# Layer-0 output projection over five slices of the contraction instead of eight

## The reference, cut to what matters

```python
Wdkv = x @ latent_w + latent_b                      # (b, t, 36): one latent, keys and values at once
q = jnp.einsum('btc,hcl->bhtl', x, Wd_w) + Wd_b[None, :, None, :]       # 16 heads of 36
scores = jnp.einsum('bhtl,bsl->bhts', q, Wdkv) / jnp.asarray(np.sqrt(d_head), dtype=x.dtype)
attn = jax.nn.softmax(jnp.where(causal[None, None, :, :], scores, -jnp.inf), axis=-1)
y = jnp.einsum('bhts,bsl->bhtl', attn, Wdkv)
z = jnp.transpose(y, (0, 2, 1, 3)).reshape(b, t, h * Wdkv.shape[-1])    # 16 * 36 = 576 columns
return z @ out_w + out_b                            # the projection that the change is about
```

## Time and profile before

| | us |
|---|---|
| median of 3 runs | 1982.03 (1975.81 to 1985.0) |
| the profiled execution | 1975.02 |
| its span, first to last instruction | 1973.3 |
| PE busy in the span | 1603.3 |
| DVE busy in the span | 1138.7 |
| time from one step of the loop to the next | 23.47 |

### The profile page before, as it was taken

How to read it: one execution, slowest core, us unless ns; L and a number is a source line. 1 busy time by engine, 2 the same in 40 slices (tenths; PEclk the granted TensorE clock), 3 DMA queues, 4 the chain that set the end, 5 groups by cost and what they waited for, 6 DMA issues and landing times. The chain is left out here.

```text
span 1973.3 us, 43060 instructions
## 1 busy us (share of the span) xinstructions
PE 1603.3 (81%) x13932; PEld 1192.2 (60%) x13933; DVE 1138.7 (58%) x2540; ACT 963.6 (49%) x2418; POOL 895.2 (45%) x1484
## 2 busy tenths in 40 slices
PE   4799999999999999989959999999999994212120
PEld 3656656565566665579948888888888883202020
DVE  3365555555555555434428999999999996211110
ACT  3354555555555455534427777877777782000000
POOL 5234444444444444434444444444444431556542
PEclk8599999999999999999979999999999997555555
DMA  8222122212212211322201111111111114323213
GB/s 228 64 40 43 41 43 49 44 40 40 40 40 41 42 41 40 63 57 67 65 24 40 42 35 39 37 37 38 37 41 35 39 35 92 70 42 60 43 19 91
DMA packets 185520, 99.83 MB, mean 51 GB/s; under 512 B 98946, under 2 KB 176323, under 8 KB 182211
## 3 DMA queue, kind: packets, MB, share of 16 engines
q1 hardware_dynamic: 173698, 83.54, 18.9%
q0 software_dynamic: 11776, 15.75, 3.9%
HBM read 64.98 MB, written 37.91 MB: 52 GB/s over the span
## 5 line engine op out<-in xcount | busy, mean ns | idle before, releaser
L611 POOL TENSOR_SCALAR_AFFINE_SELECT probs<-probs 128x512 f32<-128x512 f32 x256 | 173.9, 702 | 197.7 <-ACT probs L1444 197.5
L1444 ACT ACTIVATE probs<-bankT 128x1024 f32<-128x1024 f32 x128 | 131.0, 1023 | 221.0 <-PE bankT L1763 221.0
L893 DVE TENSOR_REDUCE mneg<-bankS 128x2 f32<-128x256 f32 x256 | 109.0, 426 | 212.6 <-PE bankS L1743 210.9
L894 DVE TENSOR_REDUCE mneg<-bankS 128x2 f32<-128x512 f32 x256 | 174.6, 682 | 0.0
L1435 ACT ACTIVATE qT<-bankA,bd 128x256 f32<-128x256 f32 x256 | 107.5, 473 | 87.7 <-PE bankA L1725 87.7
L2137 PE MATMUL bankB<-ident,xg 128*128 128x128 f32 x32 | 8.7, 427 | 173.3 <-DMA xg<-xtab,sidx 173.3
L1725 PE MATMUL bankA<-xnT,wd 128*128 128x256 f32 x512 | 148.9, 414 | 0.0
L604 POOL CAST qb<-qT 128x256 bf16<-128x256 f32 x256 | 97.1, 398 | 96.9 <-ACT qT L1435 96.7
L1777 PE MATMUL bankB<-probs,vaug 128*64 128x512 f32 x512 | 139.0, 621 | 1.2 <-POOL probs L611 0.8
L1760 PE MATMUL bankT<-qT,kT 37*128 37x512 f32 x512 | 136.9, 611 | 3.2 <-ACT probs L1446 2.0
L821 POOL DMA_INDIRECT acc<-yo,aidx x64 | 91.7, 1433 | 102.0 <-DMA acc<-yo,aidx 90.7
(11 more groups left out here) (302 smaller groups left out, 4516.0 us busy)
## 6 DMA issues: line engine op xcount, KB each, us to landing
rzb<-reciprocals SPq DMA_DIRECT2D x64, 384.0 KB, 5.4
xtab<-tab SPq DMA_DIRECT2D x32, 192.0 KB, 2.0
xs_sorted<-zeros SPq DMA_DIRECT2D x1, 4608.0 KB, 19.1
qT<-xs_sorted SPq DMA_DIRECT2D x36, 128.0 KB, 2.1
ys_sorted<-qT SPq DMA_DIRECT2D x36, 128.0 KB, 1.8
value_rows<-vrow SPq DMA_DIRECT2D x32, 128.0 KB, 1.8
vx<-value_rows SPq DMA_DIRECT2D x256, 16.0 KB, 1.9
acc<-res SPq DMA_DIRECT2D x32, 128.0 KB, 1.8
```

What stands on the lines that cost most here:

```text
L611: pool.affine_select(out=blocks, in_=blocks, compare_op=ALU.is_ge, fill=0.0, base=0, pattern=[[0, 4], [1, P]], channel_multiplier=-1).then ...
L893: dve.tensor_reduce(mneg[:, n.half, 0, :, j], bankS[:, :, 0:128], AX.X, ALU.max, negate=True)
L894: dve.tensor_reduce(mneg[:, n.half, 1, :, j], bankS[:, :, 128:384], AX.X, ALU.max, negate=True).then_inc(S["red_done"], 1)
L1444: act.activation(pT[:, g % 2].rearrange("p e j t -> p e (j t)"), bankT[:, 0:2, :], ACT.Exp, scale=SCALE0).then_inc(S["exp_done"], 1)
```

## The change

The contraction of the projection has 576 rows of weights plus one for the bias, which would fill 4.5 tiles of 128; before, it is done over 8 tiles of which 74 rows each carry something. Now it is done over 5 (`FULL`). Pairs 0 to 4 stay where they are. The rows of pairs 5, 6 and 7 (six heads) are copied by DMA, before they are normalised, from their own place into the empty rows 37 to 63 and 101 to 127 of tiles 0 to 4. `MOVES` lists six such copies, three for each half: 27 rows of three pairs, 9 rows of two pairs, and 9 rows of one pair. The weights `ow` are laid out in the same way. The bias moves to tile 4.

The inverses are laid out likewise: two broadcasts to the 37 native rows of each half (5 KB on each partition), and one for each entry of `MOVES`. So a batch now has six copies within SBUF and eight broadcasts of `rzb`, in place of two broadcasts. SP issues the copies two at a time in the round trip (`move`), and DVE waits for all 14 transfers on one semaphore (`zrows_in`). `normalise` covers 5 tiles in three instructions instead of 8 in four, and `outp` has 5 matmuls for a token tile instead of 8.

The loads of `ow` at the start stand behind those of x now and count on `w_in`, which PE waits for ahead of its loop.

```diff
+        FULL = 5
+        REST = PAIRS - FULL
+        NATIVE = (slice(0, L + 1), slice(LP, LP + L + 1))
+        W27 = LP - (L + 1)
+        MOVES = []
+        for e in range(2):
+            o = LP * e
+            MOVES.append((slice(o, o + W27), slice(FULL, PAIRS), slice(o + L + 1, o + LP), slice(0, REST)))
+            MOVES.append((slice(o + W27, o + L), slice(FULL, FULL + 2), slice(o + L + 1, o + 2 * L + 1 - W27), slice(REST, FULL)))
+            MOVES.append((slice(o + W27, o + L), slice(FULL + 2, PAIRS), slice(o + 2 * L + 1 - W27, o + 3 * L + 1 - 2 * W27), slice(REST, REST + 1)))
+        ow = sb("ow", [P, FULL, C])
...
+            def move(p, k):
+                for rows, heads, to, tiles in MOVES[2 * k:2 * k + 2]:
+                    sp.dma_start(yT[to, p.half, tiles, :], yT[rows, p.half, heads, :]).then_inc(S["zrows_in"], 16)
+
             def denominators_out(p):
                 sp.wait_ge(S["y_sb"], p.b * GROUPS + GROUPS)
                 sp.dma_start(den_d, yT[DEN:DEN + LP + 1:LP, p.half]).then_inc(S["den_out"], 16)
+                sp.wait_ge(S["zrows_in"], p.b * NZ)
+                move(p, 0)
                 sp.wait_ge(S["den_out"], p.b * 16 + 16)
                 sp.dma_start(dq[:, :], den_d.rearrange("e j t -> (e j t)").rearrange("(p k) -> p k", p=P)).then_inc(S["den_in"], 16)
+                move(p, 1)
 
             def reciprocals_out(p):
                 sp.wait_ge(S["rec_done"], p.b + 1)
                 sp.dma_start(rec_d.rearrange("e j t -> (e j t)").rearrange("(p k) -> p k", p=P), rq[:, :]).then_inc(S["rec_out"], 16)
+                move(p, 2)
 
             def reciprocals_in(p):
                 sp.wait_ge(S["rec_out"], p.b * 16 + 16)
                 for e in range(2):
-                    sp.dma_start(rzb[LP * e:LP * e + RB], rec_d[e:e + 1].to_broadcast([RB, PAIRS, T])).then_inc(S["rzb_in"], 16)
+                    sp.dma_start(rzb[NATIVE[e]], rec_d[e:e + 1, 0:FULL].to_broadcast([L + 1, FULL, T])).then_inc(S["zrows_in"], 16)
+                for rows, heads, to, tiles in MOVES:
+                    e = rows.start // LP
+                    sp.dma_start(rzb[to, tiles], rec_d[e:e + 1, heads].to_broadcast([to.stop - to.start, heads.stop - heads.start, T])).then_inc(S["zrows_in"], 16)
...
             def normalise(p, i):
                 if i == 0:
-                    dve.wait_ge(S["rzb_in"], p.b * 32 + 32)
-                rows = yT[:, p.half, 2 * i:2 * i + 2, :]
-                ins = dve.tensor_tensor(rows, rows, rzb[:, 2 * i:2 * i + 2, :], ALU.mult)
-                if i == GROUPS - 1:
+                    dve.wait_ge(S["zrows_in"], p.b * NZ + NZ)
+                tiles = slice(2 * i, min(2 * i + 2, FULL))
+                rows = yT[:, p.half, tiles, :]
+                ins = dve.tensor_tensor(rows, rows, rzb[:, tiles, :], ALU.mult)
+                if i == FULL // 2:
                     ins.then_inc(S["z_done"], 1)
...
-                for j in range(PAIRS):
+                for j in range(FULL):
                     ins = pe.matmul(bankB[:, t * C:(t + 1) * C], yT[:, p.half, j, t * P:(t + 1) * P], ow[:, j, :],
-                                    start=(j == 0), stop=(j == PAIRS - 1))
+                                    start=(j == 0), stop=(j == FULL - 1))
```

More of the change, by code:

```diff
@@ L160, in program @@
         lwr = sb("lwr", [P, LR])
-        ow = sb("ow", [P, PAIRS, C])
+        FULL = 5
[9 more added lines that the diff above has]
+        ow = sb("ow", [P, FULL, C])
         xn = sb("xn", [P, 2, 2, C])
@@ L175, in program @@
         yT = sb("yT", [P, 2, PAIRS, T])
-        rzb = sb("rzb", [P, PAIRS, T])
+        rzb = sb("rzb", [P, FULL, T])
         dq = sb("dq", [P, H * T // P])
@@ L278, in program @@
         xt_ps xt_act xt_dve rk_sb scats xnT_sb kv_ps kv_sb
-        q_ps q_sb s_ps red_done mT_ps mT_sb st_ps exp_done av_done y_sb den_out den_in rec_done rec_out rzb_in z_done out_ps xa_done cst dumped passed xs_zero rt ex0 rk_ps staged scat0 scat1 te_done xs_in0 xs_in1 w1_sb xsT_ps xsT_sb h_ps h_act h_dve
+        q_ps q_sb s_ps red_done mT_ps mT_sb st_ps exp_done av_done y_sb den_out den_in rec_done rec_out zrows_in z_done out_ps xa_done cst dumped passed xs_zero rt ex0 rk_ps staged scat0 scat1 te_done xs_in0 xs_in1 w1_sb xsT_ps xsT_sb h_ps h_act h_dve
         yt_ps yt_sb ys_out0 ys_out1 te_go w1_in pads
@@ L291, in passed @@
             eng.sem_inc(S["passed"], 1)
-        NA = 2 * 4 + 4 + 3
-        NW = 2 + 2 * KF + 1
+        NA = 2 * 4 + 4
+        NO = 2 * 4 + 1
+        NW = 2 + 2 * KF + 1 + NO
+        NZ = 16 * (len(MOVES) + 2 + len(MOVES))
         FIRST = 4
@@ L314, in _ @@
             sp.dma_start(lbr[:, L:LR], a["L0_ffn_br"].rearrange("(o l) -> o l", o=1).to_broadcast([P, E0])).then_inc(S["w_a"], 16)
[L315 to L318, removed]
             for k in range(1, len(SPANS)):
@@ L321, in _ @@
                 sp.dma_start(xa_all[:, rows, :], xv[:, rows, :]).then_inc(S[f"x_in{k}"], 16)
+            oh = a["L0_attn_out_w"].rearrange("(j e l) c -> e l j c", e=2, l=L)
+            for e in range(2):
+                sp.dma_start(ow[LP * e:LP * e + L, :, :], oh[e, :, 0:FULL]).then_inc(S["w_in"], 16)
+            for rows, heads, to, tiles in MOVES:
+                lo = rows.start % LP
+                sp.dma_start(ow[to, tiles, :], oh[rows.start // LP, lo:lo + rows.stop - rows.start, heads]).then_inc(S["w_in"], 16)
+            sp.dma_start(ow[DEN:DEN + 1, FULL - 1, :], a["L0_attn_out_b"].rearrange("(o l) -> o l", o=1)).then_inc(S["w_in"], 16)
             for e in range(2):
@@ L1032, in step @@
                     normalise(p, 2)
-                    normalise(p, 3)
             first, second = Batch(0, 0), Batch(0, 1)
@@ L1086, in _ @@
             red(Batch(1, 0), 7)
-            for k in range(GROUPS):
+            for k in range(FULL // 2 + 1):
                 normalise(first, k)
@@ L1143, in _ @@
                 tile_step(1, q, 8)
-                normalise(last, q)
+                if q <= FULL // 2:
+                    normalise(last, q)
             with dve.Fori(2, TILES // 4 - 1) as i:
@@ L1880, in _ @@
             step(second, Batch(1, 0), None, Batch(1, 1), True, ranks=True)
+            pe.wait_ge(S["w_in"], 16 * NW)
             with pe.Fori(1, LOOP) as i:
@@ L1887, in _ @@
                 outp(Batch(LOOP, 0), t, B * GROUPS)
-            pe.wait_ge(S["w_in"], 16 * NW)
             pe.wait_ge(S["te_done"], 2)
```

## The result

The changed kernel takes 2343.74 us, median of 4 runs (2336.53 to 2348.9), against 1978.92 for the kernel before (4 runs). The ratio is 1.1848, with a 95% interval of 1.1824 to 1.1872. The forecast was 2350. All of the loss is in layer 0's attention and its tail: the span grew by 369.3 us (1973.3 to 2342.6), and the first multiplication of the last batch came 371.1 us later (1238.18 against 867.11 in the earlier trace rows).

The account below looks back on a forecast made before the run. PE was taken to bound the kernel. 29 steps of 11.9 us (9.4 waiting, 2.5 clock) make 345; with 5, 7 and 11 that is 368 on 1975, and 7.0 to the median gives 2350 us; range 2200 to 2570.

Parts of the forecast that it names:

- Part 1: PE's projection: 6 of 16 matmuls go, saving 1.40 us of 3.73 for each batch.
- rival with spread rows: Native `rzb` transfers spread over a dozen engines or more: PE keeps nearly 1.4 us a step, 1939 us; chance 0.13.
- Part 2: Copy issues on SP in the round trip: hidden, nothing taken, 0.1 us as the upper bound.
- Part 3: Native `rzb` broadcasts: all 74 rows on one engine, 14.8 us, everything landed at S+24.9.
- What is late next: PE at pair 6's row maxima waits for DVE; 8.0 us from landing to next projection, step 9.4 us longer.
- The clock: PE's clock halves after its stand in nearly every step: 5 us of work at half speed loses 2.5 us.
- The sum: Whole kernel: 29 steps of 11.9 us make 345, plus 5, 7 and 11 for batches 0, 30, 31: 368 us.
- The last two batches: Batches 30 and 31: +7 us at PE's projection and +11 us, with sorted rows queueing behind the broadcasts.
- Two different engines: Each native `rzb` broadcast on its own engine: landed S+17.5, step 25.5 us, 2040 us; chance 0.03.
- Half clock all step: PE at half clock throughout each step: up to 44 us of PE work, +20 a step, 2590 us; chance 0.05.
- The crowd's price: Native `rzb` rows at 0.45 us each, 33 us in place of 14.8: 522 us more, 2870 us; chance 0.02.

Follow-up runs that it names:

- even form: The changed kernel with the two native `rzb` broadcasts to 36 rows instead of 37, plus one transfer for both denominator rows: 1936.49 us, 1935.36 when repeated.
- run without copies: The even form without the six copies of `yT` rows, six heads left out of the projection: 1930.90 us, 1938.59 when repeated.
- filled stand: The changed kernel with 24 more matmuls, product unread, where PE stands ahead of the row maxima of pair 6: 2290.25 us.
- half dose: The changed kernel with one native broadcast to 36 rows plus a transfer for its denominator row, the other still on 37: 2144.65 us.
- `RB` = 40: The kernel before with its two `rzb` broadcasts to 40 rows in place of 48: 1977.54 us, ratio 1.0001.
- `RB` = 37: The kernel before with its two `rzb` broadcasts to 37 rows in place of 48: 2599.87 us, one run.
- `RB` = 38: The kernel before with its two `rzb` broadcasts to 38 rows in place of 48: 2245.99 us, one run.

## Why the prediction was right, step by step

**Part 1, right.** The projection went from 3.73 to 2.39 us, 1.34 by these rows, and the even form's step is shorter by 1.40 in one window and 1.30 in the mean. The 43 us of the rival with spread rows are the 41 to 44 us that the even form gained in its two jobs. The change does what it was thought to do; one number of rows hides it.

**Part 2, wrong by half a microsecond a step.** I forgot the issue of `rec_out` itself, and the copies cost 0.75 us each to issue, not 0.68. `rec_out` starts at 617.02, two copies end at 618.91, and `rzb` goes out at 618.95: 1.93 us in place of 1.46. The run without copies shows that they are the cause: 1.47 us there (529.64 to 531.11). So `rzb` is issued at S+7.44, not S+6.92 (S, the start of the projection, is 611.51 here). In the even form the same delay is there (535.28 to 537.21) and costs nothing. I had called it hidden, and in this kernel it is on the path. The first two copies delay `dq` as well, by more than the 0.06 us of the forecast: it goes out 2.37 us behind the denominators (612.01 to 614.38) where 1.82 stood (521.84 to 523.66, and again 1.82 without copies). In the loop the reciprocal is not wanted sooner and this 0.55 us is hidden; at batch 30 it is not. The fence at the head of the copies was not free in one place either: for batch 31 SP sent the denominators at 1195.20 and the copies only at 1202.71, when the `rzb` of batch 30 had landed. DVE's reciprocal of that batch, at 1215.75, did not wait for `dq`, so I count nothing for it.

```profile
1195.20 0.56 SPq L358 DMA_DIRECT2D denominators<-yT  x1
1202.71 1.53 SPq L354 DMA_DIRECT2D yT<-yT  x2
```

**Part 3, right.** One engine, the same for both; 18.04 us from issue to landing against 18.0 (2.3 + 14.8 + 0.9). Before the run it rested on even shares in three transfers and on the rule that the prediction cites; 37, 38 and 40 rows have since shown even shares here.

**What is late next, right.** Landing at S+25.5 against S+24.9, nearly all of the difference from part 2. PE resumed 1.77 us behind it; I had 2.0.

**The clock, too dear.** 1.8 to 2.0 us a step, not 2.5. The fall came in the stand as I had said, but the half clock lasted for 4 us of work behind it, not 5, and was over well before the projection.

```profile
629.30:642.70 13.40, 3.94 (x18) 1.42 (x18) 3.25 (x6) 0.42 (x1) 0.90 (x2) 0.50 0.03 13
642.90:646.50 3.60, 3.60 (x28) 2.34 (x25) 2.02 (x6) 1.20 (x3) 0.00 (x0) 1.00 0.00 0
```

3.94 us of PE work at half speed lose at most 2.0.

**The sum, right, with errors that cancel.** By the starts of the first multiplication:

| | before | after | more | forecast |
|---|---|---|---|---|
| batch 0 | 142.28 | 144.53 | 2.3 | 5 |
| batch 0 to 1 | 17.58 | 34.21 | 16.6 | 11.9 |
| batches 1 to 29, 28 steps | 658.53 | 989.51 | 331.0 (11.82 each) | 333 |
| batch 29 to 30 | 21.33 | 34.47 | 13.1 | 9.9 |
| batch 30 to 31 | 27.39 | 35.46 | 8.1 | 8.1 |

A step is 11.82 us longer against 11.9, and two errors cancel in it. The run with the filled stand separates them: its mean step of 33.34 is 9.82 above 23.52, where I had 9.4 without the clock, and the clock's part is 2.0, where I had 2.5.

The two lines of batch 0 belong together, 18.9 against 16.9. Its `rzb` took 18.39 us, as forecast, but was issued at 126.14, 3.7 us sooner than before; that is not the change's doing (the last section shows it). Behind it stands a wait that I had not seen. SP issues the weights of the next stage right behind the `rzb` of batch 0, from 130.26 to 151.45, 21.2 us, where it took 11.7 before (130.70 to 142.41). The same four issues, before and after:

```profile
133.54 2.98 SPq L366 DMA_DIRECT2D wv<-in_L_attn_wv  x4
```
```profile
138.17 6.36 SPq L392 DMA_DIRECT2D wv<-in_L_attn_wv  x4
```

So the row maxima of the next batch go out at 151.69 and not at 143.27, and PE stands 3.60 us for them. In the kernel before with 37 and 38 rows the four take 9.90 and 10.43 us, in the even form 2.67, so it goes with the few engines. That SP then waits for room in its queue is my reading; no view shows the queue's depth. The forecast had such a wait only in the upper end of its range.

**The last two batches, 3 us short.** My 7 for batch 30 was counted at PE's projection, where some slack was used up; counted at the multiplication, as in the table, the same working gives 849.6 - 839.72 = 9.9, and the rest of the 18 for both, 8.1, for batch 31. For batch 30 it was 13.1; that batch 31 agrees to the decimal is luck. The landing took 17.7 us against 18.0, but the issue came later and not 1.4 us sooner: from the multiplication of batch 29 to the issue of `rzb` it is 14.56 us before, 14.65 with the filled stand, and 16.77 in the changed kernel. So the half clock accounts for 2.1 us, which I had left out here, and nothing is left of the 1.4. The copies used up most of it: DVE waits for `dq` there, so both delays of part 2 count, 0.5 us each.

```profile
1182.64 0.35 DVE L925 RECIPROCAL rq<-dq 128x32 f32<-128x32 f32 x1 [2.70 <-DMA dq<-denominators]
```

For batch 31 the forecast had PE wait for a load of sorted rows that queues behind the broadcasts. It does, for 13.28 us where 3.72 stood:

```profile
1238.47 0.45 PE L1927 MATMUL bankA<-ident,qT 128*128 128x128 f32 x1 [13.28 <-DMA qT<-xs_sorted]
```

**The rivals.** Spread rows, refuted by the two small packets. Two different engines, refuted by the half dose and by the busy share of one sixteenth. Half clock all step did not happen: it was back at 1.00 from 642.90 on. The crowd's price did not apply: 0.19 us a row alone.

## What to carry to other kernels

Before a DMA is given a new number of rows, find the largest divisor of that number up to 16. That many engines carried it in every transfer from SP whose small packets were counted here (2, 8, 37, 38, 40 and 48 rows, and 36, 27 and 9 together), and a broadcast to 37 rows took 25.0 us here where one to 48 took 6.6. If a number is awkward, split off the odd rows or carry some that nobody needs; count the small packets in the DMA view to see how many engines took part. A wait for a DMA beside idle DMA engines is the sign to look for. Look also at what the same queue issues behind the slow transfer. And where PE stands for it in every pass, as for 11 us here, the clock cost some 2 us a pass more.

## What the runs showed that I had not expected

The record of the granted clock can be wrong, and the length of a known instruction tells. In the profile of the kernel before, 36.4 to 107.9 stands at 0.50 with PE busy for 56.37 us. In that of `RB` = 40, whose instructions there are the same, it stands at 1.00 with PE busy for 56.03 us:

```profile
36.40:107.90 71.50, 56.03 (x276) 44.31 (x276) 23.26 (x85) 26.32 (x62) 21.48 (x52) 1.00 0.32 89
```

One might read that the half clock costs nothing. But the four products of a pair's queries take as long in the one as in the other, and at full clock, in the loop, they take 1.13 us. The first line is from the kernel before, the second from `RB` = 40, the third from the loop of the kernel before:

```profile
69.55 2.08 PE L1725 MATMUL bankA<-xnT,wd 128*128 128x256 f32 x4
```
```profile
71.30 2.08 PE L1725 MATMUL bankA<-xnT,wd 128*128 128x256 f32 x4
```
```profile
512.58 1.13 PE L1725 MATMUL bankA<-xnT,wd 128*128 128x256 f32 x4
```

So PE ran at half speed in both, and the recorded 1.00 is what is wrong. My use of the earlier trace rows as the upper bound of the clock's price stands.

It also tells why batch 0 moves. By these lengths PE comes to full speed at about 107.7 in the kernel before (the same in the run with the filled stand) and at about 96.7 in the changed kernel, and the latter issues the `rzb` of batch 0 3.7 us sooner. The same happens between kernels whose instructions up to there are the same: `RB` = 37 has full speed from 98.6 and issues it at 127.95, `RB` = 38 and 40 have it from about 109 and issue at 132.90 and 132.93. So a few us at the start differ from one execution to the next, whatever the kernel.
